# One store moved between queues: a convolution-and-FFN kernel's last save of its sums, issued by ScalarE instead of GpSimd

## The reference, cut to what matters

```python
xn = layernorm(x)
proj = xn @ in_proj_w + in_proj_b                 # 256 -> 768
v = proj[..., :256]
for i in range(2):
    ctrl = proj[..., (i + 1) * 256:(i + 2) * 256]
    v = fft_conv(v, implicit_filter(i))           # causal, as long as the sequence
    v = v * gated_control(ctrl, i)                # short conv, then a sigmoid gate
attn = v @ out_proj_w + out_proj_b
h = bitlinear(xn, w_fc) + gate * (xn @ v_.T @ fast_b.T @ u.T)
ffn = bitlinear(relu(h) ** 2, w_proj)             # 256 -> 1024 -> 256
out = x + attn + ffn
```

## Time and profile before

| | us |
|---|---|
| three executions | 961.53, 954.75, 962.61 |
| their median | 961.53 |
| the profiled execution | 957.39 |
| its span | 955.8 |
| mixing stage, from the barrier at L463 to the one at L815 | 371.7 to 870.4 |
| output stage | 870.4 to 955.7 |

### The profile page before, as it was taken

How to read it: one execution, slowest core, us unless ns; L and a number is a source line. 1 busy time by engine, 2 the same in 40 slices (tenths; PEclk the granted TensorE clock), 3 DMA queues, 4 the chain that set the end, 5 groups by cost and what they waited for, 6 DMA issues and landing times. The chain is left out here.

```text
span 955.8 us, 26466 instructions
## 1 busy us (share of the span) xinstructions
PE 863.9 (90%) x9972; PEld 718.4 (75%) x9973; DVE 631.3 (66%) x1025; ACT 479.1 (50%) x678; POOL 248.7 (26%) x268
## 2 busy tenths in 40 slices
PE   6846999999999973999999999999999999972995
PEld 3324888888888863888888888888888888862895
DVE  6882799898998973456555565565555655651885
ACT  5413677777777773333443343444434343334662
POOL 1022464664646601011121121111111111110111
PEclk9977899999999997999999999999999999985998
DMA  6272323324233129676778868778777687693897
GB/s 185 65 252 106 117 100 123 141 88 159 105 119 145 68 95 292 119 172 160 164 146 195 181 154 172 145 174 183 176 167 162 148 183 172 127 196 86 249 332 275
DMA packets 86705, 152.84 MB, mean 160 GB/s; under 512 B 12981, under 2 KB 62278, under 8 KB 85382
## 3 DMA queue, kind: packets, MB, share of 16 engines
q1 hardware_dynamic: 74902, 109.01, 47.2%
q0 software_dynamic: 11616, 42.21, 13.4%
q10 hardware_dynamic: 144, 1.05, 0.3%
HBM read 102.83 MB, written 49.41 MB: 159 GB/s over the span
## 5 line engine op out<-in xcount | busy, mean ns | idle before, releaser
L1080 PEld LDWEIGHTS py<-vwin,lead 64*64 64x64 f32 x5120 | 134.0, 134 | 35.8 <-issue 35.8
L965 DVE TENSOR_TENSOR r_lo<-r,r_hi 128x512 fp32r<-128x512 f32 x128 | 107.6, 840 | 78.8 <-ACT r_hi L1012 78.8
L1080 PE MATMUL py<-vwin,lead 64*64 64x128 f32 (+4 forms) x5120 | 147.8, 266 | 12.8 <-issue 12.7
L1012 ACT ACTIVATE r_hi<-r 128x512 fp32r<-128x512 f32 x128 | 80.8, 631 | 153.7 <-DVE r L960 153.7
L1009 ACT ACTIVATE r<-pf 128x512 f32<-128x512 f32 x128 | 76.5, 598 | 137.2 <-PE pf L412 132.7
L1061 PE MATMUL pp<-wproj,r_hi 128*128 128x256 f32 x512 | 135.9, 299 | 3.4 <-DVE r_lo L965 2.4
L1061 PE MATMUL pp<-wproj,r_lo 128*128 128x256 f32 x512 | 127.8, 282 | 0.0
L451 POOL TENSOR_SCALAR lead<-lead,norms 128x256 f32<-128x256 f32 x64 | 113.8, 1788 | 3.4 <-POOL norms L445 3.4
L1061 PEld LDWEIGHTS pp<-wproj,r_hi 128*128 128x128 f32 x512 | 96.9, 189 | 19.2 <-DVE r_lo L965 5.7
L611 DVE SCALAR_TENSOR_TENSOR xc<-ctrl,taps,xc 128x512 f32<-128x512 f32 x128 | 96.8, 776 | 18.8 <-ACT xc L683 18.1
L410 PE MATMUL pf<-tokens,split_a 128*128 (+1 forms) x256 | 101.3, 396 | 0.4 <-issue 0.4
(11 more groups left out here) (158 smaller groups left out, 1607.1 us busy)
## 6 DMA issues: line engine op xcount, KB each, us to landing
lead<-filters SPq DMA_DIRECT2D x128, 320.0 KB, 5.9
xnT_hbm<-split_b SPq DMA_DIRECT2D x32, 512.0 KB, 3.1
tokens<-xnT_hbm POOLq DMA_DIRECT2D x32, 512.0 KB, 7.0
lead<-in_attn_x SPq DMA_DIRECT2D x16, 512.0 KB, 3.8
gc_hbm<-xc SPq DMA_DIRECT2D x16, 512.0 KB, 2.6
xb<-in_attn_x POOLq DMA_DIRECT2D x16, 512.0 KB, 7.2
xf_hbm<-xb POOLq DMA_DIRECT2D x16, 512.0 KB, 3.8
GC<-gc_hbm SPq DMA_DIRECT2D x32, 256.0 KB, 7.4
```

The costliest lines, as they stand in the source:

```text
L965: dve.tensor_tensor(r_lo[j][:, :], r[j][:, :], r_hi[j][:, :].bitcast(F32), ALU.subtract).then_inc(r_split, 1)
L1012: act.activation(r_hi[j][:, :], r[j][:, :], ACT.Copy).then_inc(r_hi_done, 1)
L1080: last = pe.matmul(py[g % 2][q * BW:(q + 1) * BW, side, l, :, A:NB], tile[rows, q * PAIR + l, j * BW:(j + 1) * BW], vwin[g % 2][rows, q, l ...
```

## The change

The last store of the sums, of chunk 15, is taken from GpSimd's program and put at the end of ScalarE's program of the mixing stage. It moves the same 512 KB from `xb` to `xf_hbm[15]`, behind a wait for the last count of `xf_ready`, and counts up a semaphore of its own, `last_saved`. In the output stage SyncE waits for 15 stores on `xf_saved` and for `last_saved`, and ScalarE waits for `last_saved` ahead of `wo_hi`. Nothing else is altered.

```diff
@@ mix_stage, gpsimd
             save_xf(NCH - 2)
             load_xb(NCH - 1)
-            save_xf(NCH - 1)
@@ mix_stage, scalar, at its end
                 body(order, ITERS - 1, ITERS * order + ITERS - 1, True)
+            act.wait_ge(xf_ready, NCH + 1)
+            act.dma_start(xf_hbm[NCH - 1], xb[:, :, :]).then_inc(last_saved, 16)
@@ output_stage, sync
-            sp.wait_ge(xf_saved, 16 * NCH)
+            sp.wait_ge(xf_saved, 16 * (NCH - 1))
+            sp.wait_ge(last_saved, 16)
@@ output_stage, scalar
             stage(0, 0)
             stage(0, 1)
+            act.wait_ge(last_saved, 16)
             act.wait_ge(wo_in, 16 * KT)
             act.activation(wos[0][:, :, :], wo, ACT.Copy).then_inc(wo_hi_ready, 1)
@@ conv_ffn_kernel
-        xf_saved = ctx.enter_context(nc.semaphore("xf_saved"))
+        xf_saved, last_saved = (ctx.enter_context(nc.semaphore(n)) for n in ("xf_saved", "last_saved"))
```

More of the change, by code:

```diff
@@ L811, in channels, with mix_stage @@
     return m * (GPI * PAIR) + g * PAIR
-def mix_stage(nc, load_output, xf_saved, gc2_saved, x, filters, fc_hi, fc_lo, proj_t, xnT_hbm, xf_hbm, out_b, scales, flag, V, GC1, T, wfc, xm, T_loaded, w_in, xn_loaded, load_T, load_tokens):
+def mix_stage(nc, load_output, xf_saved, last_saved, gc2_saved, x, filters, fc_hi, fc_lo, proj_t, xnT_hbm, xf_hbm, out_b, scales, flag, V, GC1, T, wfc, xm, T_loaded, w_in, xn_loaded, load_T, load_tokens):
     with ExitStack() as ctx:
@@ L1118, in _, with output_stage @@
                     mixed(order, False)
-def output_stage(nc, out, load_gates, load_sum, xf_saved, ident, V, gc2, xf, wo, gc2_loaded, xf_loaded, wo_in):
+def output_stage(nc, out, load_gates, load_sum, xf_saved, last_saved, ident, V, gc2, xf, wo, gc2_loaded, xf_loaded, wo_in):
     with ExitStack() as ctx:
@@ L1411, in load_output @@
                 load_sum(sp, j, j)
-        mix_stage(nc, load_output, xf_saved, gc2_saved, x, filters, fc_hi, fc_lo, proj_t, xnT_hbm, xf_hbm, out_b, scales, flag, V, GC1,
+        mix_stage(nc, load_output, xf_saved, last_saved, gc2_saved, x, filters, fc_hi, fc_lo, proj_t, xnT_hbm, xf_hbm, out_b, scales, flag, V, GC1,
                   T, wfc, xm, T_loaded, w_in, xn_loaded, load_T, load_tokens)
-        output_stage(nc, out, load_gates, load_sum, xf_saved, ident, V, gc2, xf, wo, gc2_loaded, xf_loaded, wo_in)
+        output_stage(nc, out, load_gates, load_sum, xf_saved, last_saved, ident, V, gc2, xf, wo, gc2_loaded, xf_loaded, wo_in)
 _INS = ["attn_x", "attn_in_proj_w", "attn_in_proj_b", "attn_out_proj_w", "attn_out_proj_b", "attn_freqs",
```

## The result

The changed kernel takes 953.64 us (median of 20 runs, 950.16 to 957.61) against 962.38 (20 runs, 954.75 to 967.56): ratio 0.9912, 95% interval 0.9892 to 0.9932, so 8.5 us faster, between 6.5 and 10.4. The profiled execution took 950.16 (span 948.6) against 957.39 (955.8). Two more sets of the same kernel gave 0.9931 (0.9904 to 0.9959) and 0.9933 (0.9903 to 0.9964).

A forecast was written before the change was run, and what follows sets the result against it. It took GpSimd's 10.72 us drain to hold the barrier before the output stage. The stage starts 10.8 us earlier, but waiting for the store leaves 7.3: 959.5 - 7.3 = 952.2 us, range 947 to 958.5.

The forecast's parts named there:

- The stage starts 10.8 us earlier: Output stage's first copy at 859.65 instead of 870.45, after ScalarE's issue, a short drain and the release.
- GpSimd's drain at nothing, hidden: At the mixing stage's end: GpSimd's drain, 4.83 us behind arithmetic alone, hidden by other engines' wait for the last addition.
- Landing at 866.6, 7.7 us after issue: The 512 KB store on ScalarE's queue lands at 866.6, slowed by output-stage preloads, its issue being at about 858.95.
- the step at `wo_hi`: Output stage: ScalarE's wait for the store puts `wo_hi` at 866.7 instead of 873.97, a gain of 7.3 us.
- SyncE's first load 9 us earlier: Output stage: SyncE's first load, at 875.77 before, starts when the store has landed, 9 us earlier.
- The rest keeps the gain: Output stage from `wo_hi` on keeps its length, clock behaviour repeating, so the whole 7.3 us remains.
- a longer rest as a sign of being wrong: Output stage longer than 81.8 us from `wo_hi` to the end would show the prediction wrong.
- Rival 1: Store interleaved with the preloads, landing at 863.1, so the copies decide: gain 10.8 us, 948.7; chance 0.22.
- Rival 2: ScalarE's drain or the barrier waits for the store as GpSimd's did: gain 3.5 us, 956.0; chance 0.06.
- Rival 3: Something else holds the boundary, or full DMA stretch absorbs the earlier start: gain 0 to 2 us, about 958.5; chance 0.06.
- Rival 4: Slower: the early wait holds `wo_hi` until a store served last lands, 4.2 us later than before: 963.7; chance 0.04.
- the turning point: At the wait ahead of `wo_hi`: a store landing 15.0 us after issue or later turns the change into a loss.

The follow-up runs named there:

- pool_wait: The changed kernel with GpSimd also waiting for the last addition, then copying 16 columns of bo_row in place: 956.56 us, ratio 0.9952 to the kernel before.
- r_before: The kernel before, unaltered, run once more for a second profile: 958.31 us in one execution.
- sp_issues: The changed kernel with the last store issued by SyncE at the end of its mixing-stage program instead of ScalarE: 955.92 us, ratio 0.9941 to the kernel before.

## Why the prediction was right, point by point

- *The stage starts 10.8 us earlier.* Measured from the addition, 11.58 to 1.12: 10.46. The sum had left out 0.3 us between the end of ScalarE's issue (856.19) and the start of its drain (856.5); the drain (0.14) and the release (0.25) took what was summed.
- *GpSimd's drain at nothing, hidden.* Right as to the cost: 7.65 us, over before the addition. The reading behind it was wrong: the 4.83 us of the earlier trace rows are no cost behind arithmetic, they are the time of the arithmetic itself, beside which that drain ran; it ended 0.1 us after it (kernel before):

```profile
65.58 4.83 POOL L451 TENSOR_SCALAR lead<-lead,norms 128x256 f32<-128x256 f32 x4 [0.22 <-POOL norms L445]
```

In the mixing stage the drain ended 5.2 us behind the bias (846.02 to 851.25), and pool_wait's 5.2 us behind its copy. Of the 10.72 us in the earlier trace rows some 5 would have been there without any DMA. The change gains because GpSimd's last instruction comes early, not only because no DMA lies ahead of its drain.
- *Landing at 866.6, 7.7 us after issue.* Mis-sized: 9.3, 5.4 and 9.3. The reason was right: hardware queue q10 waited behind a full q1 as q0 had. So the step at `wo_hi` was 5.7, 9.6 and 5.7 us (15.10 less 9.39, 5.51, 9.37) for 7.3.
- *SyncE's first load 9 us earlier.* It followed at 865.24, right behind the landing; measured from the addition that is 7.5 us earlier (16.90 to 9.45), since the landing came later than summed.
- *The rest keeps the gain.* Not wholly, and the prediction had named a longer rest as a sign of being wrong. In the first profile 1.6 us were lost (83.4 us from `wo_hi` to the end, for 81.8); over all profiles of the two kernels 1.9 us (84.3 on average, for 82.4). About 1.0 of the 1.6, by an estimate, is the clock, which I had taken to repeat: from the second transposes (870.40) the first `po` matmul at a short length (0.30 us, then 0.28, instead of 0.41) came after 5.4 us, for 3.2 before. Until then `po` matmuls started every 0.21 us instead of 0.12, which over the 2.2 us more makes the 1.0. In the other profiles this was 3.4 to 5.6 us, and 3.9 in r_before. The rest can lie in VectorE's waits for loads in the last chunks: 3.4, 4.2 and 5.1 us in the changed kernel, 2.1 and 4.1 before. Two or three profiles of each don't settle how much of this comes from the change.
- *Rivals.* Rival 1, the interleaving, fell: the rule of the Trainium skill ("DMA: Bandwidth & Descriptors", "Queues, rings and completion order") of going round packet by packet is not what these rows show; q10 got nothing for over 5 us beside a full q1. Its 4.6 us to `wo_hi` came only when preloads were taken away, or when `wo_hi` no longer waited for the store. Rival 2 fell by ScalarE's drain of 0.14 us. Rival 3 fell in its first half, by the first copy at 1.12 us; of its second half, an earlier start absorbed by the loads, the 1.9 us above may be a part. Rival 4's place is real, 4.56 us of idle time, but its price stayed far from the 15.0 us of the turning point. With the Trainium skill's other rule (same page, "Issuing engines are not separate DMA queues") sp_issues agrees: the transfer didn't become faster, 9.9 us from issue to landing. The gain is larger than the 0.5 us that the prediction worked out by that rule, because it comes from GpSimd's drain.

The forecast of 7.3 us lies inside all three intervals. The profiles show 5.4 us of it at the boundary and after, the timed runs 6.4 to 8.5; the difference is within their spread, and whether the change gives anything elsewhere stays open.

There was luck in the closeness. The landing was summed 1.6 us too short in two profiles and 2.3 too long in one, and on average the step at `wo_hi` came out at 7.3 us (15.4 before, 8.1 after) with the loss behind it not foreseen. The forecast time of 952.2 is 1.4 us off the measured 953.64 because its base, 959.5, was 2.9 us below the median of 962.38, while the gain between the medians, 8.7 us, was 1.4 us larger. And one percent as the least that can be told from no change was too coarse: the interval here is 0.2% to either side.

## What to carry to other kernels

Ahead of a barrier, look for who drains last, and when that engine's last instruction can be issued: GpSimd's drain cost 5 to 11 us here, ScalarE's and SyncE's 0.1 behind the same store. The projection stage's end has the same pattern, untouched by this change: in the kernel before GpSimd's drain ends at 371.5, 1.7 us after the last other one, and in all profiles 1.6 to 3.4 us after it. No run took that away.

```profile
L463 POOLq DRAIN  x1: 5675/5675/5675, 365.8 to 365.8; - x1
...
L463 SPq DRAIN  x1: 128/128/128, 369.7 to 369.7; - x1
```

When the barrier no longer waits for a transfer, whoever reuses its buffer does; put that wait, and the buffer, where it is needed last. Prefetches ahead of a stage's end are paid for by the last store, which queues behind them.

## What the runs showed of the hardware that was not expected

- GpSimd's drain lasted 5.2 us beyond its last arithmetic in the mixing stage (pool_wait: copy over at 856.7, drain at 861.9), but 0.1 us in the setup stage, and 1.36 us in all at the kernel's end. Beyond the landing of its own DMA it lasted 2.6 to 3.0 us at this boundary in five profiles (10.72, 11.25, 11.13, 5.89 and 6.04 us in all); in the last two the end also lies 5.3 to 5.5 us behind the end of the issue, so there the landing isn't shown to matter. What sets these 5 us isn't settled; the mixing stage is one with software-queue DMAs, and this wasn't tried apart.
- A store of 512 KB on a second hardware queue moved no packet for 5 us while the first was full (issued at 855.82, first packets after 861.0), as the software queue's had moved none for 3.
